# A gated delta net on one core: head 1's scores and two projections moved ahead of head 0's first cross product

## What is computed

```python
qkv = hidden_states @ W_qkv.T                # 16 key heads, 32 value heads, 128 wide
z = hidden_states @ W_z.T
xp = jnp.pad(qkv, ((0, 0), (KS - 1, 0), (0, 0)))
mixed = silu(sum(xp[:, k:k + Sn, :] * conv_w[:, k] for k in range(KS)))   # KS = 4
# q, k (l2-normalized, each for two value heads), v; g and beta from W_a, W_b
def step(state, inp):                        # over the 64 tokens of a sequence
    qt, kt, vt, gt, bt = inp
    state = state * jnp.exp(gt)[..., None, None]
    kv = jnp.einsum('bhk,bhkv->bhv', kt, state)
    delta = (vt - kv) * bt[..., None]
    state = state + jnp.einsum('bhk,bhv->bhkv', kt, delta)
    return state, jnp.einsum('bhk,bhkv->bhv', qt, state)
# outputs: rms norm, times silu(z), then @ W_out.T and the residual
```

## Time and profile before

| | us |
|---|---|
| median of 3 runs | 1512.07 |
| lowest, highest | 1511.48, 1514.16 |
| the profiled execution | 1516.13 |
| its span in the trace | 1514.3 |

### The profile page before, as it was taken

The page is one execution under the profiler, slowest core; times in us unless marked ns, Lnnn a source line. Parts: engine busy times, 40 slices in busy tenths (PEclk is TensorE's granted clock), DMA queues, the critical chain, the costliest instruction groups (busy, mean ns, idle before and its releaser), DMA issues. The chain is left out here.

```text
span 1514.3 us, 33541 instructions
## 1 busy us (share of the span) xinstructions
PE 1409.0 (93%) x13924; PEld 975.2 (64%) x13924; DVE 1089.5 (72%) x1726; ACT 599.0 (40%) x1014; POOL 586.9 (39%) x963
## 2 busy tenths in 40 slices
PE   6999499999998868999999999999999878999999
PEld 3444278877885445777776676777667764655556
DVE  3898576688556876999898988989899645433443
ACT  2444354355324533555445545445555411111110
POOL 1021143244214645567556657755666610000000
PEclk9999799999998988999999999999999999999999
DMA  8443200110000131221222122122112205000000
GB/s 247 155 134 91 70 1 2 29 29 2 1 1 1 32 80 36 45 59 44 55 53 51 51 45 59 44 50 60 45 45 50 45 8 223 1 1 0 14 0 14
DMA packets 125959, 74.69 MB, mean 49 GB/s; under 512 B 95536, under 2 KB 107056, under 8 KB 124016
## 3 DMA queue, kind: packets, MB, share of 16 engines
q1 hardware_dynamic: 125808, 72.55, 17.9%
HBM read 54.69 MB, written 17.83 MB: 48 GB/s over the span
## 5 line engine op out<-in xcount | busy, mean ns | idle before, releaser
L1908 DVE SCALAR_TENSOR_TENSOR W<-PS,wc,W 128x504 f32<-128x504 f32 x375 | 269.4, 731 | 36.5 <-ACT W L1599 28.8
L2253 PE MATMUL PS<-HT,wgu 128*128 128x512 f32 x320 | 143.5, 592 | 0.0
L1599 ACT ACTIVATE W<-PS,wc 128x512 f32<-128x512 f32 x125 | 86.1, 690 | 119.6 <-PE PS L1284 108.9
L2387 DVE SCALAR_TENSOR_TENSOR act<-th,PS 128x512 f32<-128x512 f32 x48 | 33.0, 687 | 129.9 <-ACT th L2313 129.9
L1307 PE MATMUL PS<-wz,HT 128*128 128x256 f32 x512 | 125.0, 392 | 1.2
L1284 PE MATMUL PS<-HT,wv 128*128 128x512 f32 x252 | 122.1, 617 | 2.3 <-DVE W L1908 2.3
L1484 PE MATMUL PS<-wo,ogT 128*128 128x256 f32 x512 | 117.0, 387 | 7.3 <-DVE dl L1988 4.9
L1284 PE MATMUL PS<-HT,wkq 128*128 128x512 f32 x248 | 118.7, 621 | 3.2 <-DVE W L1908 3.2
L1484 PEld LDWEIGHTS PS<-wo,ogT 128*128 128x128 f32 x512 | 99.1, 194 | 21.9 <-DVE dl L1988 5.1
L2313 ACT ACTIVATE th<-PS 128x512 f32<-128x512 f32 x48 | 28.7, 597 | 208.2 <-PE PS L2253 208.2
L1603 ACT ACTIVATE W<-W 128x512 f32<-128x512 f32 x125 | 78.6, 629 | 74.3 <-DVE W L1908 73.0
(11 more groups left out here) (278 smaller groups left out, 2911.8 us busy)
## 6 DMA issues: line engine op xcount, KB each, us to landing
a_rows<-AT SPq DMA_DIRECT2D x16, 512.0 KB, 2.7
wk<-in_l0x_k SPq DMA_DIRECT2D x16, 384.0 KB, 5.7
wgu<-in_moe_gu SPq DMA_DIRECT2D x5, 1024.0 KB, 15.2
queries_scratch<-tts SPq DMA_DIRECT2D x32, 128.0 KB, 2.4
wkq<-in_gdn_w SPq DMA_DIRECT2D x16, 256.0 KB, 3.3
wv<-in_gdn_w SPq DMA_DIRECT2D x16, 256.0 KB, 2.8
wz<-in_gdn_w SPq DMA_DIRECT2D x16, 256.0 KB, 2.7
wo<-in_gdn_w SPq DMA_DIRECT2D x16, 256.0 KB, 2.9
```

Of the source, the lines that this page charges most:

```text
L1599: a.activation(acc[:, flows(h, q), :], PS[:, qbank(h, q), :], ACT.Copy, scale=wc[:, h % 2, 4 * c + 3:4 * c + 4]).then_inc(s["tap"], 1)
L1908: v.scalar_tensor_tensor(a0, p0, wc[:, h % 2, 4 * c + 2 - k:4 * c + 3 - k], a0, ALU.mult, ALU.add).then_inc(s["conv"], 1)
L2253: mm = pe.matmul(PS[:, 2 * (i % 2) + w, :], pack[:, k, w, :], HT[:, k, f * N:(f + 1) * N], start=(k == 0), stop=(k == DC - 1))
```

## The change

In `first`, TensorE now has projects (1, 5), scores_q(1) and scores_k(1) ahead of cross(0), and project(1, 6) between cross(0) and grow(0), where it stood after mix(0). On VectorE two taps of conv(1, 5) go ahead of norms(1), silu(1, 4) and the third tap ahead of update(0), make_A(1, ·) ahead of silu(1, 5), and keep_M(0, ·) ahead of silu(1, 6) and make_P(1, ·). On ScalarE tap(1, 5) and tanh(1, 4) go ahead of keep_X(0), and tap(1, 6) ahead of tanh(1, 5). Nothing is added or removed.

```diff
--- before.py
+++ after.py
@@ -1546,14 +1546,14 @@
                     project_z(0, 3)
                     project(1, 3)
                     project(1, 4)
-                    cross(0)
+                    project(1, 5)
                     scores_q(1)
                     scores_k(1)
+                    cross(0)
+                    project(1, 6)
                     grow(0)
-                    project(1, 5)
                     lower_cross(0)
                     mix(0)
-                    project(1, 6)
                     correct(0)
                     project(1, 7)
                     outs(0)
@@ -1745,13 +1745,13 @@
                     tanh(1, 2)
                     tap(1, 4)
                     tanh(1, 3)
+                    tap(1, 5)
+                    tanh(1, 4)
                     keep_X(0)
-                    tanh(1, 4)
-                    tap(1, 5)
+                    tap(1, 6)
                     tanh(1, 5)
                     keep_lower(0)
                     keep_Z(0)
-                    tap(1, 6)
                     tanh(1, 6)
                     swap_scale(1)
                     tap(1, 7)
@@ -2075,19 +2075,21 @@
                     silu(1, 3)
                     conv(1, 4)
                     norm_q(1)
+                    conv_tap(1, 5, 0)
+                    conv_tap(1, 5, 1)
                     norms(1)
+                    silu(1, 4)
+                    conv_tap(1, 5, 2)
                     update(0)
-                    silu(1, 4)
-                    conv(1, 5)
-                    silu(1, 5)
                     make_A(1, 0)
                     make_A(1, 1)
+                    silu(1, 5)
                     conv(1, 6)
+                    for hv in range(2):
+                        keep_M(0, hv)
                     silu(1, 6)
                     make_P(1, 0)
                     make_P(1, 1)
-                    for hv in range(2):
-                        keep_M(0, hv)
                     conv(1, 7)
                     silu(1, 7)
                     gate(0, 1)
```

## The result

| | before | after |
|---|---|---|
| median of 7 runs, us | 1511.82 | 1501.25 |
| lowest, highest | 1507.11, 1514.72 | 1498.63, 1513.32 |
| span of the profiled execution | 1514.3 | 1499.5 |

The ratio is 0.9946, with a 95% interval from 0.9922 to 0.9971: 8.2 us faster, between 4.4 and 11.8. The same kernel timed again later, against new runs of the kernel before, gave 0.9956 (0.9944 to 0.9968), 6.6 us. The forecast of 1505.4 against 1512.07 was a ratio of 0.9956. So the direction, the place and, by the ratio, the size were right.

A forecast was written before the change was run, and what follows sets the result against it. TensorE sets the pace from about 580 us; ahead of that, `dl` sets turn_out(0, 0) at 579.22. make_A's 7.2 us less 0.5 for DMA give 6.7: 1505.4 from the median of 1512.07, range 1502.5 to 1509.5.

The forecast's parts named there:

- the chain: Start-up: make_A(1, ·), a_rows and sy, substitute(1), then `dl` set turn_out(0, 0), which comes 6.7 us sooner.
- Scores: TensorE: scores_q(1) and scores_k(1) start near 533.3, ahead of cross(0), and end at 536.1 or 537.5, against 541.3.
- the two cases that I kept open: Head 1's scores on TensorE take 2.8 us at the full clock, or 4.2 us with the clock at 0.50.
- norms(1) and Ed: VectorE starts norms(1) near 537.6, behind norm_q and two taps; GpSimd's Ed ends at 542.9, before at 546.7.
- silu(1, 4): VectorE, behind norms: takes 0.7 us and holds Ed up some 0.2 by the skill's rule, or takes 1.45.
- make_A: VectorE: make_A(1, ·) ends at 543.9, between 543.6 (bound by Ed) and 544.5 (by update(0)), 7.2 us sooner.
- The DMA term: a_rows, issued beside wg and wkq, lands 0 to 3.8 us later (far end from wkq's 6.4 us landing); 0.5 taken.
- TensorE's wait "about as long as before": Ahead of turn_out(0, 0): conv(1, 7) and project(2, 3) come 6.5 us sooner too, so the wait for `dl` stays some 6 us.
- The slack that I called enough: VectorE: keep_M(0, ·) waiting for a late correct(0) costs nothing, since make_P ends before conv(1, 7) is needed; otherwise 1.6 us.
- third rival: Behind turn_out(0, 0): TensorE's clock stays high, half of 10 us gained on top, 1500.4; 7%.
- second rival: Loop over heads: its 12 waits for `dl` each grow by 0.5 us, 6 us go, 1511.4; 9%.
- The fourth, slower: TensorE stays at 0.50 clock deep into the saturated stretch; after 20 more us the kernel takes 1515.4; 3%.

The follow-up runs named there:

- e0: Changed kernel again, source unchanged, timed against new runs of the kernel before: ratio 0.9956 (0.9944 to 0.9968).
- e2: Changed kernel with make_A(1, 0) and make_A(1, 1) put back behind silu(1, 5) on VectorE: ratio 0.9953 to the kernel before.
- e5: Changed kernel plus five unused matmuls on TensorE between project(2, 3) and turn_out(0, 0): ratio 0.9933 to the kernel before.
- e3: Changed kernel with the 1 MB load of wg issued after head 1's DMAs on SyncE: ratio 0.9943 to the kernel before.
- e8: Changed kernel with wg loaded late and clear(0) ahead of substitute(1) on GpSimd: ratio 0.9930 to the kernel before.
- e10: Changed kernel with wg late, clear(0) early, two filling matmuls, and loads of wv and wz held until sy landed: ratio 0.9923 to the kernel before.
- e9: Changed kernel with wg late, clear(0) early, and two filling matmuls ahead of turn_out(0, 0): ratio 0.9925 to the kernel before.
- e6: Kernel before plus six unused matmuls on TensorE between project(2, 3) and turn_out(0, 0): ratio 0.9966 to the kernel before.
- e1: Kernel before with only make_A(1, 0) and make_A(1, 1) moved ahead of conv(1, 5) and silu(1, 5) on VectorE: ratio 0.9948.
- e7: Kernel before again, source unchanged, one execution for a second trace: 981.9 us from project(1, 4) to the end of the span; no ratio.
- e11: Kernel before, with head 1's loads of wv and wz held until sy landed: ratio 0.9994 (0.9980 to 1.0008).

## Why the prediction was right, and where a step of it failed

The forecast counted 6.7 us to turn_out(0, 0) and nothing behind it. Measured: 6.1 in the first pair of traces, 5.7 in the second (49.8 and 44.0), and 2.5 and 3.0 behind it from the clock. So the chain was right, and that the total came out at the forecast is in part luck: the DMA took more than was counted, and the clock gave back what was counted at nothing. Step by step, in distances from project(1, 4):

- **Scores.** Forecast 5.9, measured 5.96, and 2.8 us long: the clock was at 1.00, the favourable of the two cases that I kept open. Right.
- **norms(1) and Ed.** Forecast 10.2 and 15.5, measured 10.0 and 15.3. Right, and with it the claim that the two taps ahead of norms set its start.
- **silu(1, 4).** It took 0.68 us at 537.63, and GpSimd's `dd` beside it 0.78: the rule of the Trainium skill (SBUF — State Buffer, "Who interferes with whom") that the first to start goes first is the one that the trace followed here. It changed the sum by nothing: Ed ended 2.8 us behind norms(1), and 2.85 before.
- **make_A.** Forecast 16.5, measured 16.1; a gain of 7.6 for 7.2. Ed bounds it, with 0.31 us of waiting. Right.
- **The DMA term was mis-sized.** I took 0.5 out of a range of 0 to 3.8 us. From a_rows to sy it took 4.5, 4.6, 4.6 and 4.1 us in four traces (after, e0, e2, e5) in place of 2.6, so 1.4 to 2.0 more, and 3.1, 2.9 and 2.8 with wg out of the way (e3, e8, e10; 3.8 in e9). In the forecast the old traffic was gone less than 2 us after the issue and the row of wkq was the far end; the truth lay halfway. The rule of the Trainium skill (DMA: Bandwidth & Descriptors, "Issuing engines are not separate DMA queues") that transfers interleave pointed to the small end. The trace agrees that they overlap (the DMA engines were 98% busy from 541.4 to 543.4, while a_rows and wg were both under way), but the price was not at the small end.
- **substitute(1) covered that up.** It was 1.1 us shorter than in the trace of before. The second trace of before has 11.5 us as well and e6 12.5, so this is scatter and not the change.
- **The step that failed: TensorE's wait "about as long as before".** I had conv(1, 7) end near 26.1 and project(2, 3) at 39.0; they ended at 29.0 and 43.2. lower_cross waited 2.62 us for the last blocks of T, whose landing I had not put into the path, and ran at 0.50 clock; correct(0), which the forecast had end at 19.6 (547), started at 20.8 and ended at 22.8, and keep_M at 548.02 had VectorE waiting for it for 3.14 us, with project(1, 7) behind correct(0) at the low clock until 551.2, and tap(1, 7) and conv(1, 7) behind that. GpSimd's sk, which the forecast had as what conv(1, 7) waits for, ended on time (22.5 for 22.7); it was project(1, 7) that came last. The slack that I called enough was used up, and project(2, 3) ended only 2.3 and 3.1 us sooner than before (43.2 and 42.4 against 45.5), not 6.5. None of it reached turn_out(0, 0), since `dl` was later still. But the wait for `dl` shrank to 2.55 and 1.59 us, and behind these shorter waits the clock came back sooner (the first) or stayed up (the second). e2, whose TensorE was ready at 40.3, had the long wait and the low clock of the forecast.
- **So the third rival came true in part.** It had 7%: half of 10 us at the low clock, 5 us. The stretch behind turn_out(0, 0) gave 2.5 in the first trace and all of it, 3.0 to 3.9, in the second. e6 shows that the clock alone is worth that much, with turn_out(0, 0) where it was. I had dismissed it on the ground that the wait stays as long, which rested on the step above.
- **The loop took nothing back** (second rival): 5.6 us of waiting for `dl` in 12 waits, 6.7 before. The fourth, slower, did not come.

The rows of the changed kernel behind the failed step: TensorE's project(1, 7), ScalarE's tap(1, 7) and VectorE's conv(1, 7).

```profile
547.90 3.32 PE L1284 MATMUL PS<-HT,wv 128*128 128x512 f32 x4
551.26 0.69 ACT L1599 ACTIVATE W<-PS,wc 128x512 f32<-128x512 f32 x1 [3.12 <-PE PS L1284]
551.98 2.27 DVE L1908 SCALAR_TENSOR_TENSOR W<-PS,wc,W 128x504 f32<-128x504 f32 x3 [0.87 <-ACT W L1599]
```

What stays open: a_rows took 3.8 us in e9 with the same order as in e8 (2.9); wkq was issued 2.2 us ahead of it there and 2.7 to 3.0 in e3, e8 and e10, but no run tests whether that is why. The 7.1 us of sy in the first trace of the change are open too, and so is what decides whether TensorE is ready at 40.3 or at 43.2: the matmuls from lower_cross to project(1, 7) ran at the low clock for longer in some traces than in others. And from one trace of each kernel, 1 us either way at turn_out(0, 0) is scatter of sy and substitute(1).

## What to carry to other kernels

Follow the wait back to the engine that is last, and move the link of that chain that stands behind unrelated work: here the move of one pair of products on VectorE (e1) can't be told by its time from the reordering of three engines, though its trace is 3.4 us behind. Ask of a start-up wait on TensorE what the clock does behind it, since a few matmuls of filling, with nothing moved, gained 5 us. Fill no more than the wait holds: where the wait was gone, the filling itself held the next product up by 0.9 to 1.5 us. And when the runs scatter by more than the effect, compare distances from an instruction that the change doesn't touch: that takes out a start-up that varies by up to 9.6 us. It doesn't take out all: the two executions of the changed kernel, 3 us apart in total, are 0.2 apart by that measure, but the two of the kernel before are still 5.0 apart. Compare stretch by stretch, and have more than one trace of each kernel.

## What the runs showed of the hardware

- The granted clock fell to 0.50 in or behind waits of 6.33, 6.35, 4.57, 3.78 and 2.55 us ahead of turn_out(0, 0) (before, e2, e7, e11, after). Against the 6.7 us to head 2's scores at 1.00 they cost 3.9, 2.5, 3.0, 3.0 and 1.4 us in the saturated stretch behind. Waits of 1.25 to 1.59 us cost nothing in three kernels, one of 1.96 us cost 3.0 (e8). Ahead of project(2, 2), waits of 2.9 to 3.0 us left the clock up in before, e0, e6, e9 and e11, and brought it down in after, e2, e3, e5, e8 and e10.
- In all five traces with TensorE's order of before (before, e1, e6, e7, e11) mix(0) stands still for 1.6 to 2.4 us within its own matmuls, waiting for nothing that the profile shows; in the traces with the new order it doesn't. project(1, 7) behind it still waited 1.6 to 2.0 us for VectorE, so it cost nothing here; its cause is open.
